# Output store and first weights' load moved down the queue of transfers, in the body loop of a cross-attention and mixture-of-experts kernel

## The chip, the cores and the metric

The kernel runs on one core of one Trainium2 chip. The metric is the device time of one execution in microseconds (us), lower is better. A core has a matrix engine (TensorE, PE in the profile), a vector engine (DVE), a scalar engine (ACT), GpSimd (POOL) and a sync engine (SP) that here does nothing but issue transfers. Every engine runs its own instructions in order and waits on semaphores. SP's issues form one list, called SP's queue below: a wait in it holds back everything that is written after it.

## The reference

Input x has 8 batches of 512 tokens of 256 features, with a context of the same shape. In float32:

```
x = x + attention(layernorm(x), ctx)      # 16 heads of 16, softmax over 512 keys, projections wq wk wv wo with biases
h = layernorm(x)
probs = softmax((h @ Wg + bg) / 5); two best of 8 experts per token, gates = their probabilities / sum
x = x + sum over the two of gate * (gelu(h @ W1[e] + b1[e]) @ W2[e] + b2[e])     # 256 -> 512 -> 256
```

## The kernel before

**Attention.** Eight bodies (`body(i)`, one per batch i) follow a prologue. A body has four groups g of four heads, and group number u = 4i + g. For each group TensorE computes the scores twice: once for the row maxima (`score`, two groups ahead) and once transposed (`score_t`), with the maxima folded into the product through extra rows of the tile `kq[g]`. ACT takes exp into `probs`, and TensorE multiplies with the values and gets numerators and denominators (`pv`). Between these, at fixed places (group, step) written out in tables, the engines project the next batch, project the output of the batch before (`OP0` to `OP3`, added to `x_all` by DVE), route it, and scatter its rows to `xs_dram` (POOL).

**SP's queue in a body**, in order, in words: `put_max` puts a group's maxima into `kq[g]`; `load_stack` loads a group's keys and queries for the next batch; `put_o(u)` stores group u's numerators to `o_dram` and moves its denominators into `den`; `put_recip` stores the reciprocals that DVE made of them; `fetch_o` waits for that store and fetches numerators (`numT`) and reciprocals (`recT`), which DVE multiplies in `normalise`; `store_out(i - 1)` stores the attention result of the batch before (512 KB, from `x_all`) to the output; `load_w1` and `load_w2` load one expert's weights (512 KB each), `load_w2(e)` into the part of `x_all` of batch e. `load_w2(e)` therefore waits until `e + 1` output stores have landed, line 554. `store_stage` stores the high part of an expert's weights, `load_kv` and `load_x` fetch inputs two and three batches ahead.

**The last body** (i = 7, `more` false) also loads biases b2 and b1 (3 MB in all, lines 568 and 574) and the first four blocks of expert rows (`load_rows`, L611). Behind it, SP loads the high parts of five experts' second weights (`load_w2_hi`, L595, 512 KB each), stores the last numerators, and loads blocks 4 to 7, which wait until those numerators have landed (L608).

**Experts.** The tokens are now sorted by expert into 71 blocks of 128 rows. For block j TensorE does `turn_x(j)` (transposes, L1683), `hidden(j)` (L1692), `turn_h(j)` (L1701) and `output(j)` (L1710); ACT, DVE and POOL split, add biases, apply gelu and add the result to the output with an indirect transfer (L910). What gates the first blocks:

```
DVE, last body, group 3, step 6:  normalise(7, 0)  waits for recT     # then low_last, then low_xt(0)
ACT:  high_last(2, 6)     waits for load_w2(6)                        # L997, then gelu(0)
DVE:  low_last(2, 6)      waits for that, then take_h(0)
PE:   before output(0)    waits for all five load_w2_hi and low_last(2, 6)
PE:   turn_x(4)           waits for block 4 of load_rows
```

Of the kernel before, what the change touches and what calls it, by code (L numbers as in the profile page):

```python
# [15 lines left out]
B, S, D = 8, 512, 256  # L16
# [61 lines left out]
E, TOPK, HID = 8, 2, 512  # L78
# [111 lines left out]
def build(nc, x, ctx_kv, wqT, bq, wkT, bk, wvT, bv, woT, bo, wg, bg, w1, b1, w2, b2, out):  # L190
    with ExitStack() as stack:
# [232 lines left out]
        def sum_of(b):  # L424

            return x_of(b) if b < B - 1 else xg[:, :, 0:D]
# [29 lines left out]
        def _(sp):  # L456
            def load_x(b):
                sp.dma_start(x_of(b), x_tiles[:, b * NT:(b + 1) * NT, :]).then_inc(x_in[b % 3], 16)

            def load_w1(e):  # L460
                sp.dma_start(w1_sb[:, bass.ds(e, 1)], w1[bass.ds(e, 1)].rearrange("e (c p) h -> p e c h", p=P)).then_inc(w1_in, 16)

            def load_kv(b):
                if b > 1:
                    sp.wait_ge(full["V1"], b - 1)
                sp.dma_start(kvT[:, b % 2], ctx_kv[b]).then_inc(kv_in, 16)

            def load_stack(b, g, kinds="KQ"):
                if b > 0:

                    sp.wait_ge(st_full, NP * (NG * (b - 1) + g + 1))
                    sp.wait_ge(max_full, NP * (NG * (b - 1) + g + 1))
                for n, src, stored in [{"K": (0, k_dram, k_stored), "Q": (1, q_dram, q_stored)}[kind] for kind in kinds]:
                    sp.wait_ge(stored, 16 * PARTS * (2 * b + g // 2 + 1))
                    settle(sp, passed_sp)
                    for h in range(2):
                        sp.dma_start(kq[g][HALF * h:HALF * h + ROW_M, n].bitcast(F32),
                                     src[bass.ds(b, 1), g // 2, :, g % 2, :, h, :].rearrange("o d r s -> (o d) r s")
                                     ).then_inc(stack_in[g], 16)
                if b > 0:  # L480

                    sp.dma_start(kq[g][ROW_M::HALF, 1].bitcast(F32).rearrange("o r (c d) -> o (r c) d", d=D),
                                 pad[0:2, 0:D].unsqueeze(1).to_broadcast([2, 2 * S // D, D])).then_inc(stack_in[g], 16)

            def store_parts(kind, b, f):
                n, dram, order, stored = ((1, k_dram, ((0, qk_hi), (2, qk_hi), (1, qk_lo)), k_stored) if kind == "K" else
                                          (0, q_dram, ((0, qk_hi), (1, qk_hi), (2, qk_lo)), q_stored))
                for part, src in order:

                    sp.wait_ge(split_done, 8 * b + 2 * SPLIT[kind, f] + (1 if src is qk_hi else 2))  # L490
                    settle(sp, passed_sp)
                    sp.dma_start(dram[bass.ds(b, 1), f, part * DH:(part + 1) * DH].rearrange("o d g r h s -> (o d g r h) s"),
                                 src[:, n, :].bitcast(F32)).then_inc(stored, 16)

            def put_max(b, g):
                v = NG * b + g
                sp.wait_ge(done["MT"], v + 1)

                sp.dma_start(kq[g][ROW_M::HALF, 1].bitcast(F32),
                             mT[:, v % 2, :].bitcast(F32)).then_inc(m_in[g], 16)  # L500

            def put_o(u):

                b, g = divmod(u, NG)
                sp.wait_ge(o_out, u + 1)
                sp.dma_start(o_dram[u % (2 * NG)], oT[:, u % 2, :]).then_inc(o_stored[u % 2], 16)
                if b > 0:

                    sp.wait_ge(recip_stored[g // 2], 16 * b)
                lo = HALF * (g % 2)  # L510
                sp.dma_start(den[lo:lo + HALF, g // 2, :], oT[DH::2 * DH, u % 2, :]).then_inc(den_in[g % 2], 16)

            def put_recip(b, c):
                sp.wait_ge(recip_done, DC * b + c + 1)
                sp.dma_start(r_dram[c].rearrange("h (a s) -> (h a) s", a=DH), den[:, c, :]).then_inc(recip_stored[c], 16)
# [17 lines left out]
            def store_out(b):  # L533
                for t in range(NT):
                    sp.wait_ge(done[f"OP{t}"], b + 1)
                sp.dma_start(out_tiles[:, b * NT:(b + 1) * NT, :],
                             sum_of(b)).then_inc(out_done, 16)

            def keep_x(b):
                sp.wait_ge(bo_added, b + 1)  # L540
                settle(sp, passed_sp)
                sp.dma_start(out_tiles[:, b * NT:(b + 1) * NT, :], x_of(b)).then_inc(x_moved, 16)
# [8 lines left out]
            def load_w2(e):  # L551
                if e < E - 1:

                    sp.wait_ge(out_done, 16 * (e + 1))
                    sp.wait_ge(xg_done, NT * (e + 1))
                else:
                    sp.wait_ge(x_moved, 16)
                sp.dma_start(x_all[:, e * NT:(e + 1) * NT, :],
                             w2[bass.ds(e, 1)].rearrange("o (c p) d -> p (o c) d", p=P)
                             ).then_inc(w2_in if e < E - 2 else w2_late[e - E + 2], 16)  # L560
# [52 lines left out]
            def body(i):  # L613
                more = i + 1 < B
                if i + 2 < B:
                    load_kv(i + 2)
                if i + 3 < B:
                    load_x(i + 3)
                put_max(i, 1)
                if i == B - 2:  # L620
                    keep_x(B - 1)
                if i > 0:
                    put_o(NG * i - 1)
                    load_stack(i, 3)
                    if not more:
                        load_w2(E - 1)
                    put_recip(i - 1, 1)
                if more:
                    store_parts("K", i + 1, 0)
                if i > 0:  # L630
                    fetch_o(i - 1, 1)
                if more:
                    store_parts("Q", i + 1, 0)
                if not more:
                    for e in (0, 1, 2):
                        load_w1_hi(e)
                if i == 0:
                    load_stack(i + 1, 0)
                put_max(i, 2)
                if 0 < i < B - 1:  # L640
                    load_stack(i + 1, 0)
                if not more:
                    for e in (3, 4):
                        load_w1_hi(e)
                put_o(NG * i)
                if more:
                    store_parts("Q", i + 1, 1)
                    store_parts("K", i + 1, 1)
                else:
                    sp.wait_ge(stage_low, ALL_STAGED)  # L650
                    load_w1(E - 1)
                if i in STAGED:
                    store_stage(i, 0)
                put_max(i, 3)
                if more:
                    load_stack(i + 1, 1)
                else:
                    for e in (5, 6):
                        load_w1_hi(e)
                    load_b2()  # L660
                put_o(NG * i + 1)
                if not more:
                    for n in range(2):
                        load_b1(n)
                if i > 0:
                    store_out(i - 1)
                put_recip(i, 0)
                if not more:
                    sp.wait_ge(tab_done, 1)
                    sp.wait_ge(scattered, 16 * TOPK * NT * EARLY_B)  # L670
                    for j in range(EARLY_XS + 1):
                        load_rows(j)
                fetch_o(i, 0)
                if i < B - 2:
                    load_w1(i)
                if i == 0:
                    load_w1(E - 2)
                if more:
                    put_max(i + 1, 0)
                    load_stack(i + 1, 2)  # L680
                else:
                    load_w2(i - 1)
                put_o(NG * i + 2)
                if i in STAGED:
                    store_stage(i, 1)
                if 0 < i < B - 1:
                    load_w2(i - 1)
# [27 lines left out]
            for i in range(B):  # L715
                body(i)
# [1056 lines left out]
```

## Time and profile before

| | |
|---|---|
| median of 3 runs | 809.06 us (807.59 to 813.81) |
| profiled execution | 810.81 us, its span 808.9 us |
| mean granted TensorE clock | 0.992 |
| PE busy | 757.3 us, 94% of the span |
| DVE, ACT, POOL busy | 610.6, 455.7, 394.6 us |
| SP's transfers (q1) | 117.33 MB, 48.1% of the 16 transfer engines' time |
| indirect transfers of POOL (q0) | 17.09 MB, 12.0% |

The span is the time from the first to the last instruction; the execution's own time is 1.9 us longer. Busy times overlap, so only an engine near 100% can be the bound by itself. A row of a timeline gives start, duration, engine, line, operation and, in brackets, how long the engine stood idle before it and what released it.

### The profile page before, as it was taken

The numbers are of one execution on the slowest core, as the hardware profiler recorded it, in microseconds if no ns is written. First come the engines' busy times: TensorE is split into PE (matmuls) and PEld (weight loads), VectorE is DVE, ScalarE is ACT, GpSimd is POOL, SyncE is SP. The second block draws the span as 40 slices with busy tenths as digits, with TensorE's granted clock in tenths as the row PEclk, the third lists the DMA queues.
The fourth block names the chain that finished last, engine by engine and source line by source line (L and its number), as shares of the span: only waits on it lengthen the run. The fifth ranks groups of instructions, "written<-read, shape, count | busy, mean of one in ns | idle before, by whom it ended". The sixth has DMA issues, their size and how long they took to land.

```text
span 808.9 us, 16337 instructions
## 1 busy us (share of the span) xinstructions
PE 757.3 (94%) x4672; PEld 452.5 (56%) x4672; DVE 610.6 (75%) x1126; ACT 455.7 (56%) x663; POOL 394.6 (49%) x357
## 2 busy tenths in 40 slices
PE   9999999999999999999999888769999989999994
PEld 4443344444444444444444333348999879989994
DVE  6787778798798797788787787646777877766773
ACT  2066676775776776766766655843345434444441
POOL 6506143547647637728725603343453555344443
PEclk9999999999999999999999999999999999999998
DMA  6765857757757657757767556876454455454441
GB/s 220 208 180 175 224 169 219 226 170 257 209 177 251 208 191 241 202 178 229 209 176 244 163 160 239 287 266 118 77 94 78 84 129 104 71 78 74 72 70 12
DMA packets 90660, 136.24 MB, mean 168 GB/s; under 512 B 15456, under 2 KB 49216, under 8 KB 90192
## 3 DMA queue, kind: packets, MB, share of 16 engines
q1 hardware_dynamic: 76592, 117.33, 48.1%
q0 software_dynamic: 13296, 17.09, 12.0%
q8 instruction: 43, 0.70, 0.4%
q10 hardware_dynamic: 688, 0.79, 0.3%
q14 instruction: 41, 0.34, 0.1%
HBM read 71.25 MB, written 64.04 MB: 167 GB/s over the span
## 4 chain that ended last, share of the span: by engine, by line
PE 75%; issue 6%; ACT 6%; DVE 5%; DMA 4%; POOL 2%; another core or an unknown queue 0%; SPq 0%; DVEq 0%; POOLq 0%
PE ps_pv L1544 13%; PE ring L1710 10%; PE ring L1692 10%; PE ring L1531 10%; PE ring L1518 7%; PE ps_x L1575 7%; ACT probs L1022 4%; DMA out<-y_sb,xs 4%; PE ps_x L1595 4%; PE ring L1701 3%; PE ps_x L1585 3%; PE ps_x L1605 2%; DVE negm L1094 2%; PE ps_pv L1683 1%; PE ps_x L1562 1%
## 5 line engine op out<-in xcount | busy, mean ns | idle before, releaser
L1094 DVE TENSOR_REDUCE negm<-ring 128x2 f32<-128x1024 f32 x256 | 310.3, 1222 | 75.4 <-PE ring L1518 66.0
L1022 ACT ACTIVATE probs<-ring 128x1024 f32<-128x1024 f32 x256 | 260.2, 1024 | 94.1 <-PE ring L1531 73.0
L910 POOL DMA_INDIRECT out<-y_sb,xs x71 | 110.2, 1553 | 142.8 <-DMA out<-y_sb,xs 87.8
L1544 PE MATMUL ps_pv<-probs,v_aug 128*32 128x512 f32 x1024 | 137.2, 608 | 5.7 <-ACT probs L1022 5.7
L1531 PE MATMUL ring<-kq 64*128 64x512 f32 x512 | 126.2, 492 | 7.3 <-DVE negm L1094 6.1
L1518 PE MATMUL ring<-kq 64*128 64x512 f32 x512 | 106.1, 413 | 10.8 <-ACT probs L1022 6.2
L1531 PEld LDWEIGHTS ring<-kq 64*128 64x128 f32 x512 | 47.5, 183 | 110.5 <-issue 76.2
L1055 ACT CAST xsT_hi<-ps_pv 128x256 fp32r<-128x256 f32 x70 | 26.1, 373 | 132.8 <-PE ps_pv L1683 125.2
L801 POOL DMA_INDIRECT xs_dram<-xg,rows x64 | 63.5, 993 | 55.5 <-DVEq L1262 30.8
L1710 PE MATMUL ring<-w_hi,hT_hi 128*128 x284 | 85.3, 300 | 0.1
L1710 PE MATMUL ring<-w_lo,hT_hi 128*128 x284 | 80.1, 282 | 0.0
L1710 PE MATMUL ring<-w_hi,hT_lo 128*128 x284 | 79.6, 280 | 0.0
L1692 PE MATMUL ring<-w_hi,xsT_hi 128*128 x142 | 58.8, 414 | 8.9 <-DVE xsT_lo L1419 6.2
L1431 DVE TENSOR_TENSOR h_pre<-ring,b_sb 128x512 f32<-128x512 f32 x71 | 48.9, 689 | 21.8 <-PE ring L1692 20.5
L1518 PEld LDWEIGHTS ring<-kq 64*128 64x128 f32 x512 | 48.7, 186 | 27.1 <-ACT probs L1022 10.7
L841 POOL CAST qk_hi<-qk 128x512 fp32r<-128x512 f32 x28 | 17.1, 612 | 86.2 <-ACT qk L961 55.2
L857 POOL TENSOR_TENSOR v_aug<-v_flat,bv_sb 128x256 f32<-128x256 f32 x32 | 23.6, 754 | 71.9 <-PE ps_pv L1544 61.4
L1692 PE MATMUL ring<-w_hi,xsT_lo 128*128 x142 | 56.5, 398 | 0.0
L1692 PE MATMUL ring<-w_lo,xsT_hi 128*128 x142 | 56.2, 396 | 0.0
L1710 PEld LDWEIGHTS ring<-w_hi,hT_hi 128*128 128x128 f32 x284 | 53.6, 189 | 0.2 <-issue 0.2
L1710 PEld LDWEIGHTS ring<-w_lo,hT_hi 128*128 128x128 f32 x284 | 53.6, 189 | 0.0
L1710 PEld LDWEIGHTS ring<-w_hi,hT_lo 128*128 128x128 f32 x284 | 53.5, 188 | 0.0
(197 smaller groups left out, 1222.4 us busy)
## 6 DMA issues: line engine op xcount, KB each, us to landing
kq<-k_dram SPq DMA_DIRECT2D x64, 192.0 KB
kq<-q_dram SPq DMA_DIRECT2D x64, 192.0 KB
xs<-xs_dram SPq DMA_DIRECT2D x71, 132.5 KB
k_dram<-qk_hi SPq DMA_DIRECT2D x32, 256.0 KB
q_dram<-qk_hi SPq DMA_DIRECT2D x32, 256.0 KB, 2.7
o_dram<-oT SPq DMA_DIRECT2D x32, 256.0 KB
w_dram<-w_sb SPq DMA_DIRECT2D x12, 512.0 KB
w_hi<-w_dram SPq DMA_DIRECT2D x12, 512.0 KB
```

Of the source, the lines that this page charges most:

```text
L801: pool.indirect_dma_start(out=xs_dram, out_offset=bass.IndirectOffsetOnAxis(ap=rows[:, k, t:t + 1], axis=0), in_=xg[:, t, :], in_offset=No ...
L910: pool.indirect_dma_start(out=out, out_offset=bass.IndirectOffsetOnAxis(ap=xs[j % AHEAD][:, TOKEN:TOKEN + 1].bitcast(I32), axis=0), in_=y_ ...
L1022: nc.scalar.activation(probs[kt][:, 2 * jp:2 * jp + 2, :], ring[PLACE["ST", u, p] % RINGS][:], ACT.Exp).then_inc(exp_done, 1)
L1094: nc.vector.tensor_reduce(negm[:, v % 2, :, jp, kt], ring[PLACE["MX", v, p] % RINGS][:], AX.X, ALU.max, negate=True).then_inc(max_free, 1)
L1431: v.tensor_tensor(h_pre[:, j % 2, :], ps_h[j % 2], b1_sb[:, bass.ds(e, 1), :].rearrange("p o h -> p (o h)"), ALU.add).then_inc(f_h_out, 1)
L1518: mm = nc.tensor.matmul(ps[:, h, :], kq[g][lo:lo + HALF, 1, jp, kt * P:(kt + 1) * P], kq[g][lo:lo + HALF, 0, jp, :], start=True, stop=True)
L1531: mm = nc.tensor.matmul(ps[:, h, :], kq[g][lo:lo + HALF, 0, jp, kt * P:(kt + 1) * P], kq[g][lo:lo + HALF, 1, jp, :], start=True, stop=True)
L1544: mm = nc.tensor.matmul(ps_pv[2 * DH * j:2 * DH * (j + 1), :], v_aug[:, kt, HPG * g + j, :], probs[kt][:, j, :], start=(kt == 0), stop=(kt ...
L1575: mm = nc.tensor.matmul(ps[:, half], w[:, c, f * P:(f + 1) * P], act_t[:, c, half], start=(c == 0), stop=(c == DC - 1))
L1595: mm = nc.tensor.matmul(ps[:, (t % 2) * D:(t % 2 + 1) * D], numT[:, c, t * P:(t + 1) * P], wo_sb[:, c, :], start=(c == 0), stop=(c == DC - 1))
L1692: mm = nc.tensor.matmul(ps_h[j % 2], x[:, j % 2, c, :], w[:, bass.ds(e, 1), c, :].rearrange("p o h -> p (o h)"), start=(n == 0), stop=(n = ...
L1710: mm = nc.tensor.matmul(ps_y[j % 2][:, 0:D], h[:, j % 2, c, :], w[:, bass.ds(e, 1), c, :].rearrange("p o d -> p (o d)"), start=(n == 0), s ...
```

## The change

In each body of SP's queue, `store_out(i - 1)` and `load_w1(i)` (in body 0 also `load_w1(6)`) move. In bodies 1 to 6 they now stand behind `put_o(4i + 2)`, the third group's numerators, and so just ahead of `store_stage` and `load_w2(i - 1)`. In body 7 the store stands behind `fetch_o(7, 0)` and directly ahead of `load_w2(6)`. No transfer is added or removed.

```
@@ body(i)
                 put_o(NG * i + 1)
                 if not more:
                     for n in range(2):
                         load_b1(n)
-                if i > 0:
-                    store_out(i - 1)
                 put_recip(i, 0)
                 ...
                 fetch_o(i, 0)
-                if i < B - 2:
-                    load_w1(i)
-                if i == 0:
-                    load_w1(E - 2)
+                if not more:
+                    store_out(i - 1)
                 if more:
                     put_max(i + 1, 0)
                     load_stack(i + 1, 2)
                 else:
                     load_w2(i - 1)
                 put_o(NG * i + 2)
+                if more and i > 0:
+                    store_out(i - 1)
+                if i < B - 2:
+                    load_w1(i)
+                if i == 0:
+                    load_w1(E - 2)
                 if i in STAGED:
                     store_stage(i, 1)
                 if 0 < i < B - 1:
                     load_w2(i - 1)
```

## Rows read from the trace of the kernel before

**Rows 1.** Busy time of each engine in body 3 and in the later experts' blocks
```profile
core 0: us, PE busy (x) PEld busy (x) DVE busy (x) ACT busy (x) POOL busy (x), PEclk, DMA share, GB/s
247.00:309.00 62.00, 60.34 (x368) 27.07 (x366) 50.77 (x87) 42.89 (x57) 37.51 (x35) 1.00 0.68 216
563.00:809.00 246.00, 230.85 (x1593) 208.75 (x1593) 176.25 (x399) 100.17 (x195) 113.37 (x78) 0.99 0.46 78
```

**Rows 2.** Timeline of SP's queue, bodies 3 and 4: start, duration, line, transfer
```profile
261.73 0.73 SPq L536 DMA_DIRECT2D out<-x_all  x1
...
268.32 0.45 SPq L461 DMA_DIRECT2D w_sb<-in_L_ffn_W  x1
273.91 0.54 SPq L499 DMA_DIRECT2D kq<-mT  x1
...
278.72 0.38 SPq L558 DMA_DIRECT2D x_all<-in_L_ffn_W  x1
...
280.51 0.49 SPq L458 DMA_DIRECT2D x_all<-in_x  x1
287.88 0.54 SPq L499 DMA_DIRECT2D kq<-mT  x1
```

**Rows 3.** Line 536 (`store_out`) in bodies 1 to 6, its transfers
```profile
DMA to landing us min/median/max: 4.2/4.5/5.0
```

**Rows 4.** Line 558 (`load_w2`) up to 460 us, its transfers
```profile
DMA to landing us min/median/max: 5.1/5.3/6.1
```

**Rows 5.** Timeline of DVE, the reciprocals of a body's second half
```profile
295.46 0.34 DVE L1126 RECIPROCAL den<-den 128x32 f32<-128x32 f32 x1
```

**Rows 6.** Timeline of DVE, the first reciprocals of all, in body 0
```profile
86.09 0.35 DVE L1126 RECIPROCAL den<-den 128x32 f32<-128x32 f32 x1 [3.06 <-DMA den<-oT]
```

**Rows 7.** Timeline of PE just behind these
```profile
87.58 0.50 PE L1531 MATMUL ring<-kq 64*128 64x512 f32 x2 [0.57 <-DVE negm L1094]
```

**Rows 8.** Timeline of SP's queue from body 7 into the experts' blocks
```profile
511.71 0.50 SPq L536 DMA_DIRECT2D out<-x_all  x1
...
522.70 0.67 SPq L526 DMA_DIRECT2D numT<-o_dram  x1
524.34 0.59 SPq L531 DMA_DIRECT2D recT<-r_dram  x1
525.02 0.41 SPq L558 DMA_DIRECT2D x_all<-in_L_ffn_W  x1
...
526.66 4.09 SPq L595 DMA_DIRECT2D w_hi<-w_dram  x5
530.80 0.48 SPq L506 DMA_DIRECT2D o_dram<-oT  x1
...
543.16 3.66 SPq L611 DMA_DIRECT2D xs<-xs_dram  x4
```

**Rows 9.** Line 536 (`store_out`) in body 7, its one transfer
```profile
DMA to landing us min/median/max: 12.4/12.4/12.4
```

**Rows 10.** Line 515 (`put_recip`) in body 7, issued at 516.4 us
```profile
DMA to landing us min/median/max: 7.9/7.9/7.9
```

**Rows 11.** Stretches of body 7 and after, columns as in Rows 1
```profile
511.00:524.00 13.00, 9.28 (x68) 4.48 (x70) 6.31 (x25) 10.20 (x14) 1.44 (x3) 1.00 0.96 360
525.00:528.00 3.00, 2.59 (x29) 1.09 (x28) 1.45 (x8) 2.32 (x4) 0.00 (x0) 1.00 0.56 158
531.00:541.00 10.00, 5.71 (x20) 4.02 (x20) 5.18 (x8) 3.50 (x5) 6.02 (x6) 0.83 1.00 389
```

**Rows 12.** Timeline of DVE in body 7, the product with `recT`
```profile
530.83 0.69 DVE L1130 TENSOR_TENSOR numT<-numT,recT 128x512 f32<-128x512 f32 x1 [3.67 <-issue]
```

**Rows 13.** Timeline of ACT, the high part taken of `load_w2(6)`
```profile
536.79 1.05 ACT L997 CAST w_hi<-x_all 128x1024 fp32r<-128x1024 f32 x1
```

**Rows 14.** Timeline of PE: hidden(0), output(0), turn_x(4)
```profile
533.24 0.68 PE L1692 MATMUL ring<-w_hi,xsT_hi 128*128 x1 [3.13 <-DVE xsT_lo L1419]
...
543.28 0.36 PE L1710 MATMUL ring<-w_hi,hT_hi 128*128 x1
...
546.16 0.38 PE L1683 MATMUL ps_pv<-ident,xs 128*128 128x128 f32 x2
```

More of the change, by code:

```diff
@@ L664, in body @@
                         load_b1(n)
-                if i > 0:
-                    store_out(i - 1)
                 put_recip(i, 0)
@@ L673, in body @@
                 fetch_o(i, 0)
[L674 to L677, printed above, removed]
+                if not more:
+                    store_out(i - 1)
                 if more:
@@ L683, in body @@
                 put_o(NG * i + 2)
+                if more and i > 0:
+                    store_out(i - 1)
+                if i < B - 2:
+                    load_w1(i)
+                if i == 0:
+                    load_w1(E - 2)
                 if i in STAGED:
```

## The prediction

> **What bounds the kernel now.** I first compared how long TensorE is busy in each stage, then where SP's queue stands at the moment its work is needed. In body 3 TensorE works 60.34 of 62.00 us, and in the 246 us from 563 us on it works 230.85 [rows 1]. Some 12 us of the idle 15 there are the last additions after its last product, so the experts' part too is TensorE work, block after block. Two things follow. A shorter transfer can win at most 1.66 us in a body of this kind. And whatever moves the start of the experts' blocks moves the end by as much, since behind it no slack takes it up. So the place to read is the passage between the two parts, from about 511 to 546 us, where TensorE works only 5.71 of the 10 us from 531 to 541 [rows 11].
>
> **Bodies 1 to 6: what moves.** The first part is the queue up to the new place. In body 3 the store goes out at 261.73 and the w1 load at 268.32; the next instruction, `put_max(4, 0)`, goes at 273.91 [rows 2]. That one waits for maxima which TensorE and ACT make, and so do the key and query loads behind it. Between 268.77 and 273.91 the queue stands still, so taking 0.73 + 0.45 us of issues from ahead of it brings nothing forward. Only the reciprocals come sooner, and their product is made late in group 3. I take 0 for this, with the 1.66 us of idle time per body as the far bound of a gain.
>
> The second part is what is queued behind. `load_w2(i - 1)` waits until the store has landed, and the store now goes out just ahead of it. Before, it had gone 17 us earlier (261.73 against 278.72) and the wait was met on arrival. Now SP stands there for the store's landing, 4.2 to 5.0 us in bodies 1 to 6 [rows 3]; 0.7 us of it passes in issuing `load_w1` and `store_stage`. The issues behind it (w2, keys' context, x) took from 278.72 to 281.00 [rows 2]. With the store going at 278.2, where the stage's store had stood, they run from 283.2 to 285.5. The next one, `put_max(4, 1)`, goes at 287.88 for a reason of its own [rows 2], so 2.4 us are left. The three loads serve bodies further on. I take 0. If this cover is gone, `put_o(4i + 3)` is what comes late, and with it the denominators for DVE's reciprocals at 295.46 [rows 5].
>
> **Body 0.** Two w1 loads move about 7 us later. Nothing waits for the queue there, and the weights are first read in group 1 of body 1, more than a group of 15.5 us (62.00 / 4) later. 0.
>
> **Body 7, the gain.** The store (128 x 1024 x 4 bytes = 0.52 MB) goes out at 511.71, behind 3 MB of biases, and lands 12.4 us later, at 524.1 [rows 8, 9]. The reciprocals' store is issued at 516.4 and takes 7.9 us, so it lands at 524.3, just after [rows 10]. `recT` waits for it and is issued at 524.34 [rows 8]. I read this as a backlog, served in order: the transfer engines were busy 0.96 of the time at 360 GB/s from 511 to 524 [rows 11]. Without the 0.52 MB ahead, the reciprocals' store lands 0.52 / 0.360 = 1.4 us sooner. But `numT` is issued until 523.37 [rows 8], so `recT` can go at 523.5, a gain of 0.85 us. DVE stands 3.67 us for it before the product at 530.83 [rows 12]. Behind that product in DVE's order come `low_last` and `low_xt(0)`, for which hidden(0) waits at 533.24 [rows 14]. So hidden(0) starts 0.85 us sooner (bounds: 0 if the landing is latency alone, 1.4 if all of it is passed on).
>
> **Body 7, the loss.** The store now goes at 524.1, after `recT`, and `load_w2(6)` must wait for it. Bounds of this wait: 4.2 us, the quickest landing of rows 3, and 12.4 us, that of rows 9. I take 5.0, the slow end of rows 3, since those stores too had a few hundred KB ahead and not 3 MB. The load then goes at 529.1 where it went at 525.02 [rows 8]: 4.1 us later (bounds 3.3 and 11.5). It lands 5.1 to 6.1 us after that [rows 4], by 535.2. ACT reads it at 536.79 [rows 13], directly behind other work, or at 535.9 when that comes 0.85 us sooner. So gelu(0) is not held, and this step costs 0.
>
> But everything behind it in the queue is later by the same 4.1 us: the numerators of group 30, the five `load_w2_hi` that were issued from 526.66 to 530.75, the last numerators at 530.80 [rows 8]. From the w2 load on that is 0.52 + 0.26 + 2.62 + 0.26 = 3.67 MB. POOL's eight scatters (1.09 MB) run from 528.06 to 538.5 beside them. From 531 to 541 the transfer engines were full at 389 GB/s [rows 11], and before, from 525 to 528, they moved only 158 GB/s [rows 11]: w2 data started about 3 us after its issue. With the issue at 529.1 that is 532.1. By then POOL has moved about 0.42 MB, and 3.67 + 0.67 = 4.34 MB remain: 11.2 us at 389 GB/s, to 543.3, against 541.0 before. The transfers end 2.3 us later.
>
> What waits for them: output(0) needs the last `load_w2_hi`. The last numerators were known to have landed at 543.16, when `load_rows(4)` goes [rows 8]; their 0.26 MB take 0.7 us, so the weights had landed at about 542.4, 0.9 us before output(0) at 543.28 [rows 14]. At 2.3 us later that is 544.7, a loss of 1.4 us, and the 0.85 us gained at hidden(0) ends in this wait. Then turn_x(4): its block goes out at 543.16 and is used at 546.16 [rows 8, 14], so it needs at most 3.0 us. Issued at 545.5 it may hold turn_x(4) until 548.5, 2.3 us later than before, or, if it lands in 2 us, not beyond the 1.4. I take the middle, **+1.9 us in all**.
>
> Here a rule speaks. The trace's stores of 0.52 MB landed in 4.2 to 5.0 us [rows 3]. The Trainium skill (DMA: Bandwidth & Descriptors, section "Anatomy of one DMA — SWDGE (gpsimd) path") gives some 2.0 us fixed, mostly the receipt of the last write, plus bytes over 436 GB/s; for POOL's kind of transfer, and SP's is another kind. By it the store would land in 3.2 us, an estimate from that page, and the total would be about +1 us in place of +1.9. The trace's longer times decide, and the sum keeps to them. The same section says that a wait is held by the issuing engine ahead of the transfer, which is why it would speak against this change: a store and its wait side by side cost SP the whole receipt.
>
> **Sum.** 810.81 + 0 (bodies) + 0 (gelu) + 1.9 = 812.7 us for the profiled execution. The median of the runs, 809.06, lies 1.75 us below it, so I predict 811.0.
>
> **Rivals.**
> *Gain kept.* The transfers fill the idle capacity at 525 to 528 and end no later, and hidden(0) starts 0.85 to 1.4 us sooner. TensorE's granted clock was 0.83 from 531 to 541, after TensorE had stood 3.13 us [rows 11, 14]. If the shorter idle time keeps it at 2.4 GHz, 1.7 us more come back. Result -0.85 to -3.1, so 806 to 808. For it: 158 GB/s of 389 used at 525 to 528. Against it: SP stands at the store's wait just while the engines could move w2_hi.
> *Slow store in body 7.* The store lands as in rows 9, after 12.4 us. This decides from a landing of about 6.7 us on: later than 530.8 plus 6.1 the w2 load reaches ACT after 536.9 and holds gelu(0). At 12.4 the load goes at 536.5, and 3.67 MB at 389 GB/s take 9.4 us from 539.5, to 549: 8 us later than 541, plus up to 1.7 us for a half clock in the longer idle time. Result +8 to +10, 817 to 819, slower. For it: it did happen once. Against: that was behind 3 MB of biases, done by 524.
> *Late denominators in every body.* If the store takes 12.4 us in bodies 1 to 6, `put_max(i + 1, 1)` goes at 293 and not 287.88, and the denominators behind it land about 298, by the body 0 case in which DVE stood 3.06 us and TensorE lost 0.57 [rows 6, 7]. DVE would then stand some 2.5 us per body, and TensorE lose between 0.4 and 2.2, in six bodies +2.5 to +13. It begins at a landing of about 7.4 us (5.0 + 2.4); all six landings of rows 3 are below.
>
> **Chances.** Less than 1%, 8 us, can't be told from no change. The forecast (0 to +5, so 809 to 814) has 0.75; the gain kept 0.13; the slow store 0.06; late denominators 0.03; something unseen 0.03. Only the middle and upper part of the slow cases, and a part of the unseen, pass 1%: faster 0.03, same 0.90, slower 0.07. The range takes in the gain (806) and, above, the forecast with a half clock in the new idle time (+1.7) and a wait of the store up to 7 us: 810.9 + 1.7 + 2 = 815.
>
> **What would show it.** Output store of body 7 at about 524.1 and `load_w2(6)` about 5 us behind it; DVE's product with `recT` some 0.9 us sooner; TensorE idle ahead of output(0), at about 543, ended by a transfer; `load_rows(4)` near 545.5; the distance from body to body still 62.0 us, with SP's next `put_max` unmoved against the body. I'd be wrong if bodies stretch beyond 62.0, or if the first output comes sooner than before in spite of later `load_w2_hi`.

## The result

The changed kernel takes 814.52 us in the median of 20 runs (811.33 to 820.05), the kernel before 810.76 us in 20 runs beside it (807.59 to 815.35). The ratio is 1.0051, interval 1.0033 to 1.0070: about 4.1 us slower (2.7 to 5.7), less than 1%. The forecast was +1.9 us; the loss came out at about twice that. The 814.52 us lie inside the stated range (806 to 815), near its upper end and just above the forecast's own span of 809 to 814. Of the 3.5 us between the 811.0 predicted and the 814.5 measured, 1.7 us are the kernel before, whose median was 809.06 us in three runs and 810.76 in twenty. A second comparison gave less, 1.0018 (0.9986 to 1.0049), below. Four executions of the experiments' sessions, of 1430, 1183, 821 and 821 us, were slow ones and enter no ratio.

The profiled execution of the changed kernel has a span of 811.7 us against 808.9. Line numbers past 690 are two higher in it. First body 3, in the table of stretches, columns as in [rows 1]:

```profile
247.00:309.00 62.00, 60.30 (x367) 26.99 (x366) 50.78 (x88) 42.91 (x57) 37.51 (x36) 1.00 0.69 215
```

TensorE's busy time is that of [rows 1] but for 0.04 us. This execution runs 1.2 us late by 37 us already, in the prologue that the change doesn't touch, and still 1.1 to 1.3 us late at most places up to about 485 us. In the first half of body 7 only 0.5 us of that are left (the products that started at 507.00 before start at 507.47). So some 2.4 us of the +2.8 us of span arise from body 7 on, and the rest is chance. SP's queue in body 3 to 4:

```profile
278.19 0.39 SPq L506 DMA_DIRECT2D o_dram<-oT  x1
278.63 0.61 SPq L511 DMA_DIRECT2D den<-oT  x1
279.41 0.40 SPq L536 DMA_DIRECT2D out<-x_all  x1
279.85 0.51 SPq L461 DMA_DIRECT2D w_sb<-in_L_ffn_W  x1
280.48 0.92 SPq L581 DMA_DIRECT2D w_dram<-w_sb  x1
283.39 0.37 SPq L558 DMA_DIRECT2D x_all<-in_L_ffn_W  x1
...
284.44 0.43 SPq L458 DMA_DIRECT2D x_all<-in_x  x1
289.02 0.54 SPq L499 DMA_DIRECT2D kq<-mT  x1
```

The w2 load now stands behind the store and goes 4.0 us after it. The queue is free again at 284.9, and the next `put_max` goes at 289.02, 1.14 later than in [rows 2], which is how late this execution is there. Who waited for whom in SP's queue from 130 to 460 us (total us, times, longest), and the landing of these stores:

```profile
SPq L558 <- DMA out<-x_all: 11.0, 5, 2.8
```
```profile
DMA to landing us min/median/max: 4.0/4.3/5.5
```

SP stood 2.2 us a body for the store, and in the same stretch DVE waited for no transfer. DVE takes the second reciprocals at 296.61 with no idle time ahead, 1.15 after [rows 5]:

```profile
296.61 0.34 DVE L1128 RECIPROCAL den<-den 128x32 f32<-128x32 f32 x1
```

Now body 7 and the passage to the experts, SP's queue, to be laid beside [rows 8]:

```profile
523.41 0.67 SPq L526 DMA_DIRECT2D numT<-o_dram  x1
524.18 0.59 SPq L531 DMA_DIRECT2D recT<-r_dram  x1
524.94 0.41 SPq L536 DMA_DIRECT2D out<-x_all  x1
530.71 0.40 SPq L558 DMA_DIRECT2D x_all<-in_L_ffn_W  x1
...
532.34 2.52 SPq L595 DMA_DIRECT2D w_hi<-w_dram  x5
...
546.47 3.65 SPq L611 DMA_DIRECT2D xs<-xs_dram  x4
```

Between 525.35 and 530.71 the queue stands still. The store's transfer in body 7, where [rows 9] had 12.4:

```profile
DMA to landing us min/median/max: 5.7/5.7/5.7
```

And TensorE, with what it waited for, beside [rows 14]:

```profile
534.65 0.49 PE L1694 MATMUL ring<-w_hi,xsT_hi 128*128 x1 [1.56 <-issue]
...
544.49 0.36 PE L1712 MATMUL ring<-w_hi,hT_hi 128*128 x1 [0.82 <-DMA w_hi<-w_dram]
...
548.48 0.44 PE L1685 MATMUL ps_pv<-ident,xs 128*128 128x128 f32 x2 [0.95 <-DMA xs<-xs_dram]
```

Output(0) waits 0.82 us for a high part and turn_x(4) 0.95 us for its block. Neither wait stands in the profile before. Output(0) is 1.2 us later than before, turn_x(4) 2.3, in both cases with the 0.5 us of chance in it. DVE takes the product with `recT` without waiting:

```profile
530.27 0.69 DVE L1132 TENSOR_TENSOR numT<-numT,recT 128x512 f32<-128x512 f32 x1
```

That is 0.56 us before its time in [rows 12], although this execution came into body 7 about 0.5 us late. TensorE's clock must be read with this pair. TensorE has two clock levels here, and the granted clock in the rows is 1.00 at the upper one (2.4 GHz) and 0.50 at the lower one (1.2 GHz). In the profile before, part of 534 to 538 us had the lower level, in the changed kernel's none:

```profile
534.00:538.00 4.00, 2.99 (x9) 1.98 (x9) 0.56 (x2) 1.47 (x3) 3.09 (x4) 0.65 1.03 418
```
```profile
534.00:538.00 4.00, 2.34 (x10) 1.77 (x11) 0.52 (x2) 1.43 (x3) 3.09 (x4) 1.00 1.06 416
```

The first of the two is the kernel before, the second the changed one, whose own slow stretch fell a little earlier (granted 0.87 from 515 to 534 us), where ACT's and TensorE's work ran up to 2.9 us late and the wait for the high parts hid it. So this one pair blurs the cost, and the pair in the experiments below shows it barer.

### The profile page after: what moved, and what is told of

It is laid out like the page before. It is cut to its first block, busy times and chain, and to the rows that moved or that the text cites. A ratio compares the mean times of both kernels' runs of the same rounds, so it can differ in the third digit from the quotient of the medians.

```text
span 811.7 us, 16337 instructions
## 1 busy us (share of the span) xinstructions
PE 758.8 (93%) x4672; PEld 451.4 (56%) x4672; DVE 611.9 (75%) x1126; ACT 455.7 (56%) x663; POOL 394.6 (49%) x357
## 4 chain that ended last, share of the span: by engine, by line
PE 71%; DVE 7%; DMA 7%; ACT 6%; issue 5%; POOL 2%; another core or an unknown queue 1%; SPq 1%; DVEq 0%; POOLq 0%; ACTq 0%
PE ps_pv L1546 13%; PE ring L1712 10%; PE ring L1694 9%; PE ring L1533 9%; PE ring L1520 7%; PE ps_x L1577 7%; ACT probs L1024 4%; DMA out<-y_sb,xs 4%; PE ps_x L1597 3%; PE ring L1703 3%; PE ps_x L1587 3%; DVE negm L1096 2%; PE ps_x L1607 2%; PE ps_x L1564 1%; PE ps_pv L1685 1%
```

## The experiments

All times are ratios to the kernel before, run in turn with it on one chip. There were three such sessions; a time in us is compared within one only. In the first (body 7 only, bodies only, wait alone, three high parts in the wait) the kernel before took 800.11 us, in the second (one high part in the wait, the three earlier orders) 812.62, in the third (the changed kernel again, one high part again, products in the wait) 812.1.

**Where: body 7 or the other bodies?** The change was cut in two. Only body 7:

```diff
-                if i > 0:
+                if more and i > 0:
                     store_out(i - 1)
                 ...
                 fetch_o(i, 0)
+                if not more:
+                    store_out(i - 1)
```

> Only the move of body 7; bodies 0 to 6 as before. Theory A (the loss is made in body 7, where the load of w2(6) and all behind it waits for a store just issued): the whole change, about +4 us (+0.5%) against the kernel before, and in the trace load_w2(6) near 530.7 and not 525.0, the wait of TensorE for w_hi ahead of output(0) and for the block of turn_x(4). Theory B (part of it comes from the bodies, whose SP queue now stands for each store's landing): clearly less than +4 us here, and the rest in the kernel that moves bodies 0 to 6 alone. Theory C (the profile's +2.8 us is chance, since 1.2 us of it are there in the prologue already): no difference beyond the interval.

Only bodies 0 to 6 (from the changed kernel):

```diff
+                if not more:
+                    store_out(i - 1)
                 put_recip(i, 0)
                 ...
                 fetch_o(i, 0)
-                if not more:
-                    store_out(i - 1)
```

> Only the moves of bodies 0 to 6; body 7 as before. Theory A: 0, within 1 us (0.1%), bodies 62.0 us apart, though SP stands 4 to 6 us ahead of each load_w2. Theory B: +1 to +3 us, with longer bodies or DVE waiting for denominators. Theory C: 0.

Measured: body 7 alone 1.0055 (1.0032 to 1.0078), the bodies alone 0.9994 (0.9967 to 1.0020). That is the whole loss against none. In the kernel with the bodies alone SP stood for the stores just as in the whole change:

```profile
SPq L558 <- DMA out<-x_all: 11.1, 5, 2.8
```

Theories B and C fall. The two profiles, taken in one session, are also the cleanest pair for the passage. SP's queue and TensorE's wait, first with the bodies moved only (store at its old place), then with body 7 moved only:

```profile
502.26 0.52 SPq L536 DMA_DIRECT2D out<-x_all  x1
...
514.03 0.59 SPq L531 DMA_DIRECT2D recT<-r_dram  x1
514.71 0.41 SPq L558 DMA_DIRECT2D x_all<-in_L_ffn_W  x1
...
532.39 3.67 SPq L611 DMA_DIRECT2D xs<-xs_dram  x4
```
```profile
534.51 0.44 PE L1685 MATMUL ps_pv<-ident,xs 128*128 128x128 f32 x2 [0.93 <-DMA xs<-xs_dram]
```
```profile
513.04 0.59 SPq L531 DMA_DIRECT2D recT<-r_dram  x1
513.80 0.42 SPq L536 DMA_DIRECT2D out<-x_all  x1
519.39 0.40 SPq L558 DMA_DIRECT2D x_all<-in_L_ffn_W  x1
...
535.55 3.65 SPq L611 DMA_DIRECT2D xs<-xs_dram  x4
```
```profile
533.85 0.36 PE L1712 MATMUL ring<-w_hi,hT_hi 128*128 x1 [3.42 <-DMA w_hi<-w_dram]
```

`recT` goes 1.0 us sooner, the w2 load 4.7 us later, the rows of block 4 3.2 us later, and TensorE waits 3.42 us for the high parts, all at once and not in two pieces. In the other profile output(0) ran at 530.53 without a wait, but turn_x(4) already waited 0.93 us for block 4. The kernel before has the same body 7, so in an execution in which nothing else makes TensorE late it should have this wait too (inferred, not seen in a profile of its own); in [rows 14] TensorE was late itself, in part by the lower clock, and did not wait. With no slack at turn_x(4), the 3.2 us of delay of block 4 reach TensorE whole: turn_x(4) runs at 538.28 and not 534.51, 3.8 us later, of which some 0.6 us is left for the clock step below. (Of the two profiled executions the first, 797.42 us, is the fastest of its kernel's runs and the second, 804.49 us, the median of its own.) Behind the 3.42 us of idle time the clock fell here (granted 0.59 over four us), as it had not in the changed kernel's profile:

```profile
535.00:539.00 4.00, 4.00 (x18) 3.32 (x18) 1.44 (x4) 0.30 (x1) 1.06 (x1) 0.59 0.34 78
```

The delay doesn't end there. Around 550 us DVE waits for the additions of earlier blocks to the output, 5.1 us in two waits against 2.6 in the partner, and TensorE then waits for DVE:

```profile
552.33 0.49 PE L1694 MATMUL ring<-w_hi,xsT_hi 128*128 x1 [1.44 <-DVE xsT_lo L1421]
```

The partner has no such wait, and at 556 us this execution is 5.7 us behind it. Part of that is this one pair's chance, for the medians of the two kernels differ by 4.0 us.

**What: the idle wait or the bytes?** The wait alone, in the kernel before, with all transfers at their old places:

```diff
                 else:
+                    sp.wait_ge(o_in[0], 32 * B)
                     load_w2(i - 1)
```

> The kernel before in every order, but load_w2(6) also waits until recT has landed (530.8 us in the profile of before), so the queue stands still some 5.8 us with no byte moved. Theory A1 (the wait costs): nearly the whole loss, +3 to +4.5 us. Theory A2 (the bytes cost): below +1 us, since the store keeps its early place.

And the changed kernel with its wait filled, by three high parts or by one (`for e in (4,)`):

```diff
+                put_o(NG * i + 2)
                 if not more:
-                    load_w2(i - 1)
-                put_o(NG * i + 2)
+                    for e in (4, 2, 3):
+                        load_w2_hi(e)
+                    load_w2(i - 1)
```

> As the changed kernel, but in body 7 the store is followed by put_o(30) and the loads of three high parts (experts 4, 2, 3), and only then by load_w2(6) and the last two high parts. The same bytes, but the queue does not stand still while the store lands. Theory A1 (the idle wait costs): the transfers end 2 to 3 us sooner than in the changed kernel, the waits ahead of output(0) and turn_x(4) go, and the time is within 1 us of the kernel before, unless load_w2(6), now behind 1.5 MB more, holds gelu(0), which would show as ACT waiting ahead of its w_hi cast; that would leave +2 to +4 us. Theory A2 (the 0.52 MB that now fall behind 524 us cost, not the wait): no better than the changed kernel, +4 us.

> As the changed kernel, but put_o(30) and one high part (expert 4) go out in the wait, ahead of load_w2(6). Theory A1 (the idle wait costs, and what follows it in the queue sets the end): between the kernel before and the changed one, +1.5 to +3 us against before, since the transfers end about 1.5 us sooner than in the changed kernel and load_w2(6) is only 0.5 MB later, so gelu(0) is held by at most 2 us. Rival (what counts is the delay of gelu(0), as in the kernel with three loads in the wait): worse than the changed kernel, above +4.5 us.

The wait alone costs 1.0034 (1.0016 to 1.0052), 2.7 us, with the order of all transfers unchanged. It stood 4.1 us here and not the 5.8 expected (recT landed sooner): w2 at 518.90 and block 4 at 534.87:

```profile
514.21 0.59 SPq L531 DMA_DIRECT2D recT<-r_dram  x1
518.90 0.39 SPq L558 DMA_DIRECT2D x_all<-in_L_ffn_W  x1
...
534.87 3.66 SPq L611 DMA_DIRECT2D xs<-xs_dram  x4
```

Theory A2, under 1 us, is outside the interval; the size is just under A1's. Its trace has no wait of TensorE for a transfer: in that execution the lower clock (last section) had made TensorE itself late, so here the ratio has to decide and not the trace. This kernel's runs also had a lower mean granted clock than the others (0.988 against 0.992), so part of the 2.7 us could be the clock. The table at the end of the next experiment compares runs of like clock, and there the wait alone still costs 2.8 us. The clearer case against A2 is the kernel with one high part in the wait, which follows: it has the store at the changed kernel's place, and so the same bytes behind 524 us. With three high parts in the wait the ratio was 1.0037 (1.0013 to 1.0061). The time did not come back, for the reason that had been named: the queue's wait is gone (block 4 at 531.86), but w2, behind 1.5 MB more, holds gelu(0), and TensorE stands for it:

```profile
530.12 0.97 PE L1705 MATMUL ring<-ident,h_act 128*128 128x128 f32 x4 [4.72 <-ACT h_act L1071]
```

With one high part the ratio was 1.0009 (0.9978 to 1.0040); turn_x(4) waited 0.5 us for block 4 in its trace. This was below the +1.5 to +3 us expected, and the interval was wide, so it was run again beside the changed kernel:

> The changed kernel itself, beside the two below on the same chip. All theories: +0.3% to +0.7% against the kernel before.

> The kernel with put_o(30) and one high part in the wait, again. Theory A1 (the queue's idle wait is the cost): +0 to +0.2% against the kernel before, and clearly below the changed kernel. Rival (its first result near zero was the chip's scatter): the same as the changed kernel.

The changed kernel gave 1.0018 (0.9986 to 1.0049) in that session, less than the 0.3% expected, and one high part in the wait 0.9999 (0.9970 to 1.0028). Their medians are 813.91 and 811.11 us. The order is the expected one, but the two intervals overlap, so that this version is better than the changed kernel rests on the traces as much as on the times. In its second trace:

```profile
524.52 0.41 SPq L536 DMA_DIRECT2D out<-x_all  x1
...
526.17 0.66 SPq L595 DMA_DIRECT2D w_hi<-w_dram  x1
530.09 0.39 SPq L558 DMA_DIRECT2D x_all<-in_L_ffn_W  x1
...
544.34 3.65 SPq L611 DMA_DIRECT2D xs<-xs_dram  x4
```

The rows of block 4 go at 544.34, against 546.33 in the changed kernel's trace of the same session, and TensorE waits for neither transfer in this execution.

**Is the rest of the size a lower clock behind the new idle time?** Three products fill TensorE's wait:

```diff
                     if j == 1:
+                        pe.wait_ge(f_ht_out, 1)
+                        for n in range(3):
+                            nc.tensor.matmul(ps_y[0][:, 0:D], xgT[:, 0, 0:P], xgT[:, 0, 0:D], start=True, stop=True)
                         pe.wait_ge(w2_hi_in, 16 * (E - 3))
```

> The changed kernel with three products of 128x128 by 128x256 ahead of the wait for the high parts (into the bank that output(0) overwrites), so that TensorE is not idle there; they take about 1.5 us in all. Question: is the excess of the measured +4.1 us over the predicted +1.9 us a half clock granted after TensorE's new idle time? If yes: the stretch at half clock after the wait is rarer, and the time 0.5 to 1.5 us below the changed kernel. If the excess is the waits themselves: the same as the changed kernel, or up to 1 us above it.

Measured 1.0041 (1.0015 to 1.0067), no better than the changed kernel beside it. The trace shows why it doesn't settle the matter: this execution had other waits, 2.9 us for gelu(0)'s result and still 2.1 us for the high parts.

```profile
PE ring L1703 <- ACT h_act L1069: 2.9, 1, 2.9
PE ring L1712 <- DMA w_hi<-w_dram: 2.1, 1, 2.1
PE ps_pv L1685 <- DMA xs<-xs_dram: 0.8, 1, 0.8
```

The profiles of the changed kernel itself, with waits of 0.8 to 1.0 us, show no lower clock behind them either (granted 1.00 from 534 to 560 us in both). So the products had nothing to win there in a run of that kind, and bought nothing in the times; how often the long wait with a clock step behind it comes, no trace says.

The mean granted clock that every run lists says more. If the excess were a lower clock, the changed kernel's runs would show one. They don't: 0.991 for body 7 only against 0.992 for the kernel before, and 0.989 for the changed kernel in the third session against 0.988. Medians of the runs with a mean clock of 0.991 or more, in us, with the number of runs (few, and chosen after the fact):

| session | kernel before | other kernels |
|---|---|---|
| first | 800.10 (24) | body 7 only 803.65 (6), bodies only 800.10 (7), wait alone 802.89 (5), three high parts 802.91 (8) |
| second | 809.41 (10) | one high part 811.17 (4) |
| third | 810.11 (9) | changed kernel 812.82 (5), one high part 810.91 (7), products 814.42 (6) |

The loss stands at the high clock too: 3.5 us for body 7 only, 2.7 us for the changed kernel, 2.8 us for the wait alone. A lower clock is not needed to explain it. For one high part in the wait 0.8 and 1.8 us remain, so that version wins back a part, and perhaps not all.

**Can the passage be made shorter?** Three orders of body 7 of the kernel before that relieve the backlog of 511 to 524 us: b2 and half of b1 behind `load_w1(7)`; the output store ahead of the biases; and the first with the store ahead of the two w1 high parts.

```diff
                     load_w1(E - 1)
+                    load_b2()
+                    load_b1(0)
                 ...
-                    load_b2()
                 put_o(NG * i + 1)
                 if not more:
-                    for n in range(2):
-                        load_b1(n)
+                    load_b1(1)
```

> The kernel before, but in body 7 the load of b2 and of the first half of b1 (2 MB) go out behind load_w1(7), some 15 us sooner, into a stretch where the transfer engines are busy 4% of the time. The store keeps its place. Theory A (body 7's backlog holds the denominators, then the reciprocals' store and recT): -1 to -3 us against the kernel before; denominators no longer 4 us late for DVE, the store lands in 5 to 7 us and not 12. Rival (the passage is set by issues and by the five high parts from 526 us on, not by the backlog): 0, within 1 us.

```diff
                         load_w1_hi(e)
+                    store_out(i - 1)
                     load_b2()
                 ...
-                if i > 0:
+                if more and i > 0:
                     store_out(i - 1)
```

> The kernel before, but in body 7 the output store goes out ahead of the 3 MB of biases. The other direction of the change: Theory A: the store's landing is met long before load_w2(6) comes, as before, so -0.5 to +0.5 us; the denominators get 0.5 MB more ahead of them, up to 1.4 us of DVE's wait, which may cost +1. Rival (the store's place in itself moves the time, whatever waits for it): a gain of 1 us or more.

The third has the edit of the first, and `store_out(i - 1)` ahead of `for e in (5, 6): load_w1_hi(e)`:

> Both: biases b2 and half of b1 behind load_w1(7), and the output store ahead of the two w1 high parts of body 7. Theory A: as with the biases early alone or 0.5 us better, -1 to -3.5 us against the kernel before. Rival (issues set the passage): 0, within 1 us.

Ratios: 0.9991 (0.9958 to 1.0024), 0.9986 (0.9955 to 1.0017) and 0.9997 (0.9965 to 1.0028). None differs from the kernel before, and the gain that I expected of the biases failed. The first's trace says where it went, at least in part. DVE's wait for the denominators was 1.5 us, the store landed in 8.1 us, block 4 went at 539.23, some us ahead of the 542.49 of the one-high-part kernel in the same session. But SP now waits for TensorE, whose tiles the five high parts overwrite (waits of SP's queue, 500 to 560 us):

```profile
SPq L595 <- PE ps_pv L1544: 2.7, 2, 2.4
SPq L595 <- PE ring L1531: 2.4, 1, 2.4
```

and sooner transfers had little to end: in the passage the kernel before's profile has no wait of TensorE for a transfer, and that of the kernel with the bodies alone only the 0.93 us for block 4. A gain of that size is within the intervals of these three ratios (0.3% is 2.4 us) and would not show.

## Why the prediction was right, and where its size was off

**Bodies 1 to 6 cost nothing: right.** The store's landing was put at up to 5.0 us, giving back the queue at 285.5 with 2.4 us to spare; it came back at 284.9 in a run 1.1 us late, with 4.1 us to spare. The bodies alone measured 0.9994. The late denominators did not happen; its condition, a landing of 7.4 us, was never met (largest 5.5 us in the changed kernel's trace). **Body 0: right**, by the same experiment.

**The gain at `recT`: right for the transfer, too large for TensorE.** 0.85 us sooner was predicted from issue times; it was 1.0 us in the pair of one session. DVE's product came 1.4 us sooner (518.01 for 519.44), but hidden(0) only 0.3 us (521.54 for 521.85), and not the 0.85 us that the prediction passed on to it. The reading of the 12.4 us landing as a backlog held as well: the store lands in 5.7 us at its new place. As predicted what was gained ended in the later wait, so the size did not matter.

**The wait for the store: right in kind, mis-sized.** I took 5.0 us from the store's issue to the w2 load, from the slow end of [rows 3]. It was 5.8 (524.94 to 530.71), 5.9 in the changed kernel's second trace, 5.6 in the body 7 kernel and 6.3 in the one with products. The w2 load was 4.7 us late and not 4.1.

**The end of the transfers: mis-sized.** From 4.1 us I worked out 2.3 us, counting that POOL's scatters would use the gap. The pair shows 3.2 us for the rows of block 4. The 2.3 us came from laying a computed end (543.3) beside an observed one (541.0). The same sum for the kernel before, 3.67 + 1.09 MB at 389 GB/s from 528.0 us on, ends at 540.3, so like for like the delay was 3.0 us. That, and the store's wait that was 0.6 us longer, is the error.

**The stall of TensorE: right in both places, and the term that was off most.** Predicted were 1.4 us ahead of output(0) and a total between 1.4 and 2.3 at turn_x(4), of which I took the middle. The changed kernel's profile has 0.82 and 0.95 us of waits, the body 7 kernel 3.42 us in one. Against its partner output(0) is 3.3 us later (533.85 to 530.53) and turn_x(4) 3.8. The step that failed is the slack: I read 0.9 us ahead of output(0) and up to 0.9 us ahead of turn_x(4) off the profile before, in which TensorE ran partly at the lower clock from 534 to 538 us (0.65) and so came late itself. From hidden(0) to output(0) it took 10.0 us there and 8.7 us in the profile of the kernel with the bodies alone, whose turn_x(4) had no slack but a wait of 0.93 us. A third place, around 550 us, was not in the sum at all. The clock step behind the new idle time is not needed for the size: of the three profiles with this order of body 7 and nothing added only one had it, and runs of like clock show the loss without it. **What would have been better:** to compare computed ends with computed ends, and to read slack from a stretch without a clock step, or to take it as 0, which gives +3.0 us from the same rows.

**The rule.** By an estimate from the Trainium skill (DMA: Bandwidth & Descriptors, section "Anatomy of one DMA — SWDGE (gpsimd) path"), whose figures are for the other kind of transfer, the store would have landed in 3.2 us and the sum been about +1. At the changed places the traces show 4.0 to 6.3 us, so the trace's number was the one to use, and the measured loss lies on the far side of it. That a wait side by side with its transfer costs the issuing queue the whole landing, the traces of the changed kernel show: SP stands still from 525.35 to 530.71.

**Gelu(0) not held: right** (ACT's cast of the w2 tile at 536.82, where [rows 13] had 536.79), but closer than it looked: one high part more ahead of it was free, with three TensorE waited 4.72 us. And it was held once in the changed order itself: in the trace with the products the store took 6.3 us, ACT waited 1.8 us for the w2 load, and TensorE 2.9 us for gelu(0). The prediction had put that border at a landing of about 6.7 us.

## What to carry to other kernels

A transfer and the wait for its landing should not stand side by side in an issuing queue; put what does not depend on it, of about its landing time, in between. Here that won back a part of the loss, perhaps all of it. The same wait cost nothing in six bodies, where the queue had time to spare (4.1 us in the one shown), and 0.2 to 0.5% in the seventh, where all behind it was needed at once: price a queue's stall at the place where its last item has the least slack. Slack of this kind is one-sided: three orders meant to make the transfers sooner gave nothing that could be measured, since no more than 0.9 us of waiting for them had been there to win. And slack read from one profile holds for that execution only: an engine that happened to be late there hides a wait that other executions have.

## What the hardware showed that was not expected

Stretches at TensorE's lower level (1.2 GHz) come at different places in executions of nearly the same program, and not only behind its idle time at the passage. With the wait alone one lay from 519 to 527 us, and with the store ahead of the biases from 523 to 531 us, where TensorE was busy 7.30 of the 8 us:

```profile
519.00:523.00 4.00, 4.00 (x28) 1.27 (x28) 2.58 (x9) 2.05 (x2) 0.49 (x1) 0.50 0.74 165
523.00:527.00 4.00, 3.27 (x13) 0.89 (x12) 0.99 (x2) 1.83 (x3) 3.39 (x3) 0.50 1.03 407
```
```profile
523.00:531.00 8.00, 7.30 (x40) 2.00 (x38) 4.52 (x14) 5.34 (x6) 1.29 (x1) 0.50 0.83 259
```

The kernel with the bodies alone had none between 519 and 543 us. Such a stretch makes two profiles of one pair differ by a microsecond or two (1.4 us between hidden(0) and output(0), above). And the kernel before took 800.11 us in one session and 812 in two others (one of these on the same chip), a difference of 12 us and three times the effect studied, so only ratios within a session say anything here.
